# One-core graph network layer: the last edges moved into the last chunk, and a tail in five parts whose residual is doubled and summed in PSUM

## The reference

```python
msg = x[src] + edge_attr
agg = jax.ops.segment_sum(msg, dst, num_segments=N)
h = jax.nn.relu(agg @ W1 + b1) @ W2 + b2
mu = jnp.mean(h); var = jnp.mean((h - mu) ** 2)            # over everything
h = (h - mu) * jax.lax.rsqrt(var + EPS) * ln_w + ln_b
mean = jnp.mean(h, axis=0); sub = h - gn_ms * mean          # over the nodes
h = sub * jax.lax.rsqrt(jnp.mean(sub ** 2, axis=0) + EPS) * gn_w + gn_b
out = layernorm(x + (gelu(h) + x))                          # per node, over 128 features
```

## Time and profile before

| | |
|---|---|
| median of 3 runs | 765.46 us (765.35 to 767.17) |
| the profiled execution's own time | 766.76 us |
| its span in the trace | 764.9 us |
| TensorE busy | 686.3 us, 90% of the span |
| VectorE busy | 637.0 us, 83% |
| ScalarE busy | 429.0 us, 56% |
| GpSimd busy | 101.3 us, 13% |
| mean granted clock of TensorE | 0.962 of full speed |

### The profile page before, as it was taken

The page is one execution under the profiler, slowest core; times in us unless marked ns, Lnnn a source line. Parts: engine busy times, 40 slices in busy tenths (PEclk is TensorE's granted clock), DMA queues, the critical chain, the costliest instruction groups (busy, mean ns, idle before and its releaser), DMA issues.

```text
span 764.9 us, 25427 instructions
## 1 busy us (share of the span) xinstructions
PE 686.3 (90%) x9447; PEld 624.5 (82%) x9447; DVE 637.0 (83%) x1074; ACT 429.0 (56%) x968; POOL 101.3 (13%) x68
## 2 busy tenths in 40 slices
PE   1975999999999999999999999999999999989640
PEld 1964888999889998899988999889998889968530
DVE  5786989899898998989989899898998989335684
ACT  0934466655666556664566645756457564234475
POOL 2043210111101111011110112101111011000000
PEclk9986999999999999999999999999999999989975
DMA  7957465256652566525665255662556626260006
GB/s 171 298 189 247 145 196 183 97 177 214 200 185 88 181 210 205 180 89 184 206 209 187 79 190 198 209 193 75 194 193 209 202 72 199 76 168 0 0 0 167
DMA packets 88984, 123.60 MB, mean 162 GB/s; under 512 B 8572, under 2 KB 84446, under 8 KB 88763
## 3 DMA queue, kind: packets, MB, share of 16 engines
q1 hardware_dynamic: 82220, 116.30, 47.5%
q0 software_dynamic: 5744, 5.38, 2.6%
q10 hardware_dynamic: 1000, 1.65, 0.8%
HBM read 119.23 MB, written 4.03 MB: 161 GB/s over the span
## 4 chain that ended last, share of the span: by engine, by line
PE 75%; ACT 11%; DVE 6%; issue 3%; DMA 3%; DVEq 1%; ACTq 0%; SPq 0%; POOLq 0%
PE bank L800 39%; PE bank L765 17%; PE bank L713 9%; ACT counts L586 6%; PE bank L850 3%; PE bank L860 3%; PE bank L727 2%; ACT below L530 2%; DMA begins<-listed,tile_slot 2%; DMA agg<-in_dst_dram 1%; ACT pool_m L669 1%; DVE pool_m L1087 1%; DVE x_lo L1028 1%; PE bank L742 1%; PE bank L887 1%
## 5 line engine op out<-in xcount | busy, mean ns | idle before, releaser
L586 ACT CAST counts<-bank 128x490 fp32r<-128x490 f32 x600 | 320.5, 606 | 239.0 <-PE bank L765 235.9
L800 PE MATMUL bank<-counts,x_hi 128*128 128x250 f32 x1225 | 307.7, 291 | 8.7 <-ACT counts L586 8.6
L800 PE MATMUL bank<-counts,x_lo 128*128 128x250 f32 x1225 | 292.8, 279 | 0.0
L800 PEld LDWEIGHTS bank<-counts,x_hi 128*128 128x128 f32 x1225 | 230.9, 189 | 14.4 <-ACT counts L586 14.4
L1087 DVE TENSOR_TENSOR pool_m<-value_row,turned_lo 128x3328 bf16<-128x3328 bf16 (+1 forms) x125 | 229.1, 1833 | 12.0 <-PE bank L765 10.8
L800 PEld LDWEIGHTS bank<-counts,x_lo 128*128 128x128 f32 x1225 | 232.4, 190 | 0.0
L765 PE MATMUL bank<-pool_m 128*128 128x98 bf16 x3125 | 194.9, 210 | 7.8 <-DVE pool_m L1087 7.7
L765 PEld LDWEIGHTS bank<-pool_m 128*128 128x128 bf16 x3125 | 158.5, 99 | 27.2 <-issue 11.6
L1087 DVE TENSOR_TENSOR pool_m<-value_row,turned_key 128x2548 bf16<-128x2548 bf16 (+1 forms) x125 | 179.6, 1437 | 0.0
L713 PE MATMUL bank<-edges,onehot 128*32 128x128 f32 x3228 | 121.6, 285 | 5.1 <-DMA edges<-in_edge_attr_dram 3.0
L479 POOL DMA_INDIRECT near<-listed,row_slot x27 | 53.6, 1987 | 501.1 <-DVE row_slot L1049 459.5
(11 more groups left out here) (154 smaller groups left out, 442.0 us busy)
## 6 DMA issues: line engine op xcount, KB each, us to landing
edges<-in_edge_attr_dram SPq DMA_DIRECT2D x134, 768.0 KB, 6.1
out_dram<-pool_m SPq DMA_DIRECT2D x6, 512.0 KB
agg<-in_dst_dram SPq DMA_DIRECT2D x1, 768.0 KB
agg<-in_src_dram ACTq DMA_DIRECT2D x1, 768.0 KB
listed<-agg ACTq DMA_DIRECT2D x1, 768.0 KB
begins<-listed,tile_slot POOLq DMA_INDIRECT x28, 4.1
near<-listed,row_slot POOLq DMA_INDIRECT x27, 4.3
pool_m<-in_L_gnn_W_dram SPq DMA_DIRECT2D x2, 128.0 KB, 2.7
```

The source lines that it names most:

```text
L586: nc.scalar.copy(counts[:, :, at:at + NODES], cps[k % RING][:, 0:NODES * NT].rearrange("p (n q) -> p q n", q=NT)).then_inc(banks_free, 1)
L800: last = nc.tensor.matmul(sps[:, 0:CHUNK], part[:, q, :], counts[:, q, at:at + CHUNK], start=(q == 0 and part is x_hi), stop=(q == NT - 1 ...
```

## The change

- The last two groups of edges and the fast path's check are put between the 49 pairs of products of the last chunk (`finish_edges`). VectorE makes their masks before the check's counts, and adds both groups before the last chunk.
- The last part of the edge features, and the last tile of the output, are transferred in two pieces each.
- x is not loaded again. TensorE multiplies `x_hi` and `x_lo` by a diagonal matrix of twos (`double`) into a ring of seven PSUM banks, and adds the transposed gelu onto it: a matmul with `is_transpose=True` and `start=False` in place of `nc.tensor.transpose`. VectorE takes the statistics straight from PSUM (`measure`), and `finish` is gone.
- The layernorm's scales are made in five parts (blocks 0 to 2, 3 to 5, 6 to 8, 9 to 10, 11 to 12). GpSimd raises to the power -0.5, and makes the shifts; ScalarE scales blocks 0, 2, 4, 5, 6, 7, 9 and 11, VectorE blocks 1, 3, 8, 10 and the last tile, reading PSUM, and SyncE writes block by block.
- In the affine, GpSimd's power stands in place of ScalarE's square root and VectorE's reciprocal. The statistics of the first 24 chunks are joined first and the last chunk's are taken from PSUM; the chain of one-column operations is rearranged.

```diff
 BLOCK = 4
+RINGED = 7
+ACT_SCALES = {7: (0,), 8: (2,), 9: (4,), 11: (5,), 12: (6, 7, 9, 11)}
+DVE_SCALES = {6: (1,), 7: (3,)}
+DVE_LAST = (8, 10)
+BY_ACT = sum(ACT_SCALES.values(), ())
+BY_DVE = sum(DVE_SCALES.values(), ()) + DVE_LAST
+PARTS = ((0, 3), (3, 6), (6, 9), (9, 11), (11, 13))
+EVEN_LAST = 96
...
-        ops = [banks[4], sps, banks[0], banks[1]]
+        ys = [banks[i] for i in (4, 5, 7, 0, 1, 2, 3)]
+        twice = counts[:, 0, 0:P]
...
-                sp.dma_start(edges[0:REST_P, 2 + k, 0:HP], edge_rest[:, k * HP:(k + 1) * HP]).then_inc(tail_loaded, 16)
+                for a, b in ((0, REST_EVEN), (REST_EVEN, REST_P)):
+                    sp.dma_start(edges[a:b, 2 + k, 0:HP], edge_rest[a:b, k * HP:(k + 1) * HP]).then_inc(tail_loaded, 16)
...
-            sp.dma_start(xs[:, 0:NT - 1, :], x[0:(NT - 1) * P, :].rearrange("(t p) d -> p t d", p=P)
-                         ).then_inc(xs_loaded, 16)
-            sp.dma_start(xs[0:LAST, NT - 1, :], x[(NT - 1) * P:N, :]).then_inc(xs_loaded, 16)
...
+            def wait_scaled(k):
+                if k in BY_ACT:
+                    sp.wait_ge(act_out_ready, BLOCK * (BY_ACT.index(k) + 1))
+                else:
+                    sp.wait_ge(out_ready, BLOCK * (BY_DVE.index(k) + 1))
...
+            for k in range(BLOCKS):
+                wait_scaled(k)
+                sp.dma_start(out[k * BLOCK * P:(k + 1) * BLOCK * P, :].rearrange("(t p) d -> p t d", p=P),
+                             xs[:, k * BLOCK:(k + 1) * BLOCK, :]).then_inc(out_stored, 16)
+            sp.wait_ge(out_ready, BLOCK * len(BY_DVE) + 1)
+            for a, b in ((0, EVEN_LAST), (EVEN_LAST, LAST)):
+                sp.dma_start(out[(NT - 1) * P + a:(NT - 1) * P + b, :], xs[a:b, NT - 1, :]).then_inc(out_stored, 16)
...
+            pool.wait_ge(power_ready, 1)
+            for n, (base, to) in enumerate(((st[:, 3:4], st[:, 4:5]), (st[:, 9:10], st[:, 9:10]))):
+                pool.wait_ge(roots_in, n + 1)
+                pool.tensor_tensor(to, base, half_power[:, 0:1], ALU.pow).then_inc(roots_out, 1)
+            for n, (a, b) in enumerate((a * BLOCK, min(b * BLOCK, NT)) for a, b in PARTS):
+                total, scale, half = lnsum[:, a:b], rstd[:, a:b], half_power[:, 0:b - a]
+                pool.wait_ge(ln_stats, b)
+                pool.tensor_tensor(total, lnstats[:, a:b, 1], lnstats[:, a:b, 4], ALU.add).then_inc(sums_made, 1)
+                pool.wait_ge(sums_made, 2 * n + 1)
+                pool.tensor_tensor(total, total, half, ALU.mult).then_inc(sums_made, 1)
+                pool.wait_ge(sums_made, 2 * n + 2)
+                pool.wait_ge(roots_in, n + 3)
+                pool.tensor_tensor(scale, scale, half, ALU.pow).then_inc(roots_out, 1)
+                pool.wait_ge(roots_out, n + 3)
+                pool.tensor_tensor(lnshift[:, a:b], total, scale, ALU.mult).then_inc(scales_ready, 1)
...
-            for k, (a, b) in enumerate(((st[:, 4:5], turn_ps[:, 1:2]), (st[:, 9:10], st[:, 9:10]))):
-                act.wait_ge(root_in, k + 1)
-                nc.scalar.activation(a, b, ACT.Sqrt, bias=st[:, 21:22]).then_inc(root_out, 1)
...
+            def scale_block(k):
+                act.wait_ge(scales_ready, 1 + max(i for i, (a, b) in enumerate(PARTS) if a <= k))
+                for t in range(BLOCK):
+                    at = k * BLOCK + t
+                    nc.scalar.activation(xs[:, at, :], ys[k % RINGED][:, t * P:(t + 1) * P], ACT.Identity,
+                                         scale=rstd[:, at:at + 1], bias=lnshift[:, at:at + 1]).then_inc(act_out_ready, 1)
...
+            for k in range(BLOCKS + 1):
+                width = BLOCK * P if k < BLOCKS else LAST
+                if k >= 2:
+                    act.wait_ge(out_turned, k - 1)
+                nc.scalar.activation(gelu[:, k % 2, 0:width], h[:, k * BLOCK * P:k * BLOCK * P + width],
+                                     ACT.Gelu_apprx_tanh, scale=st[:, 10:11], bias=st[:, 12:13]).then_inc(act_ready, 1)
+                for done in ACT_SCALES.get(k, ()):
+                    scale_block(done)
...
+            def finish_edges(q):
+                if q in (4, 8):
+                    k = (4, 8).index(q)
+                    begin_half(FULL - 1, k, edge_loaded[k], 16 * (GPC + USES[k] * PAIRED + 2))
+                    sum_half(k, 0, k)
+                if q == 16:
+                    turn_sums(FULL - 1, 0)
+                if q in (24, 28):
+                    k = (24, 28).index(q)
+                    begin_half(FULL, k, tail_loaded, 64)
+                    sum_half(2 + k, 1, k, subs=1)
+                if q == 34:
+                    turn_sums(FULL, 1)
+                if q == 38:
+                    pe.wait_ge(ones_ready, 1)
+                    pe.wait_ge(cover_in, 1)
+                    pe.wait_ge(keys_ready, 2 * CHUNKS)
+                    nc.tensor.matmul(turn_ps[:, 0:TURNS + 2], ones, st[:, COVER:COVER + TURNS + 2], start=True, stop=True
+                                     ).then_inc(cover_summed, 1)
...
+            def double(k):
+                if k >= RINGED:
+                    done = k - RINGED
+                    if done in BY_ACT:
+                        pe.wait_ge(act_out_ready, BLOCK * (BY_ACT.index(done) + 1))
+                    else:
+                        pe.wait_ge(out_ready, BLOCK * (BY_DVE.index(done) + 1))
+                width = BLOCK if k < BLOCKS else 1
+                for part in (x_hi, x_lo):
+                    nc.tensor.matmul(ys[k % RINGED][:, 0:width * P], twice,
+                                     part[:, k * BLOCK:k * BLOCK + width, :].rearrange("p t d -> p (t d)"),
+                                     start=(part is x_hi), stop=False, skip_group_check=True)
...
+            def turn(k):
+                pe.wait_ge(act_ready, k + 1)
+                width = BLOCK * P if k < BLOCKS else LAST
+                for t in range(0, width, P):
+                    rows = min(P, width - t)
+                    last = nc.tensor.matmul(ys[k % RINGED][0:rows, t:t + P], gelu[:, k % 2, t:t + rows], ident[:, :],
+                                            start=False, stop=True, is_transpose=True, skip_group_check=True)
+                last.then_inc(out_turned, 1)
...
+            pe.wait_ge(twice_ready, 1)
+            for k in range(3):
+                double(k)
             for k in range(2):
                 pe.wait_ge(mean_in, k + 1)
                 nc.tensor.matmul(turn_ps[:, k:k + 1], ones, st[:, k:k + 1],
-                                 start=True, stop=True, skip_group_check=True).then_inc((mean_summed, root_in)[k], 1)
-            def turn(u, count, free):
-                pe.wait_ge(act_ready, count)
-                if free is not None:
-                    pe.wait_ge(y_ready, free)
-                for t in range(BLOCK):
-                    last = nc.tensor.transpose(ops[u][:, t * P:(t + 1) * P], gelu[:, u % 2, t * P:(t + 1) * P],
-                                               ident[:, :])
-                last.then_inc(out_turned, 1)
-            for u in range(OPS):
-                turn(u, u + 1, None)
-            with pe.Fori(1, BLOCKS // OPS) as it:
-                for u in range(OPS):
-                    turn(u, it * OPS + (u + 1), it * OPS + (u + 1 - OPS))
-            pe.wait_ge(act_ready, BLOCKS + 1)
-            pe.wait_ge(y_ready, BLOCKS + 1 - OPS)
-            nc.tensor.transpose(ops[0][0:LAST, 0:P], gelu[:, 0, 0:LAST], ident[:, :]).then_inc(out_turned, 1)
+                                 start=True, stop=True, skip_group_check=True).then_inc(mean_summed, 1)
+            pe.wait_ge(hidden_ready, CHUNKS * HC)
+            pe.wait_ge(h_ready, CHUNKS)
+            for k in range(3, RINGED):
+                double(k)
+            for k in range(BLOCKS + 1):
+                if k >= RINGED:
+                    double(k)
+                turn(k)
...
-            dve.memset(st[:, 21:22], EPS)
+            for k in range(2):
+                mark_lead(FULL - 1, k)
+            add(FULL - GPC, FULL % GPC, base_of(FULL - GPC), CHUNKS)
+            put(FULL - 1)
+            for k in range(2):
+                mark_lead(FULL, k)
...
+            for g in range(FULL - 1, GROUPS):
+                add(g, g % GPC, base_of(g))
...
             flag = dve.value_load(flag_i[0:1, 0:1], min_val=0, max_val=1)
-            add_chunk(CHUNKS - 1, FULL - 1, 0)
+            add_chunk(CHUNKS - 1, GROUPS, 0)
             dve.wait_ge(chunk_added, CHUNKS + 1)
-            for g in range(FULL - 1, GROUPS):
-                add(g, g % GPC, base_of(g))
-            dve.wait_ge(edges_added, GROUPS + 2)
...
+            dve.tensor_scalar(twice, ident[:, :], 2.0, None, ALU.mult).then_inc(twice_ready, 1)
+            step(dve.memset(joined[:, 0:1], float((CHUNKS - 1) * CHUNK)))
+            dve.memset(half_power, -0.5).then_inc(power_ready, 1)
...
-            keep(CHUNKS - 1, 0, CHUNKS)
-            dve.wait_ge(h_stats, CHUNKS)
...
```

(65 more changed lines are left out.)

146 lines of the change are left out of this document (18 added, 128 removed).

## The result

The changed kernel takes **753.93 us** (4 runs, 753.40 to 756.05) against 765.41: a ratio of 0.985, with a 95% interval of 0.9826 to 0.9873. That is 11.5 us gained where 16.3 were forecast. The profiled execution took 756.05 us, with a span of 754.2. That is 10.7 less than the 764.9 of the kernel before.

| stretch | before | after | forecast for after |
|---|---|---|---|
| start to the last chunk's first product | 654.63 | 658.52 | 654.63 |
| from there to the layers' first product | 19.12 | 17.04 | 16.22 |
| the layers | 45.8 | 43.15 | 42.9 |
| the layers' end to the first gelu | 7.34 | 7.66 | 7.0 |
| first gelu to the span's end | 38.0 | 27.83 | 27.8 |

The account below looks back on a forecast made before the run. After 654 us it saw TensorE bounding last chunk and layers, a VectorE chain before gelu, and VectorE the tail. Gains of 2.9 + 2.9 + 0.3 + 10.2 = 16.3 us off 765.46 gave 749.2 us, range 744.5 to 753.5.

Parts of the forecast that it names:

- Step 1: Last chunk: with the last edges inside it, the layers start at 670.85 instead of 673.75, -2.9 us.
- Step 2: Layers: TensorE, idle for only 0.8 us before them, runs at 2.4 GHz from their start, -2.9 us.
- Step 3: Affine, layers' end to first gelu: table load moved ahead, powers of 0.4 us on GpSimd, 7.0 us against 7.3, -0.3 us.
- Step 4: Tail, first gelu to the span's end: ScalarE bounds it, 27.8 us against 38.0, -10.2 us.
- If GpSimd's rows pass 1 us: Sign that the forecast is wrong: a GpSimd operation longer than 1 us in the trace.
- the other two: Signs of being wrong: TensorE waits inside the last chunk, or VectorE scales last by over 1 us.
- The clock at the layers' start: Rival: TensorE's clock falls there all the same, +2.9 us, 752.1 us; chance 0.12.
- at 0.27: Rival, tail: ScalarE's scales from PSUM cost 0.27 us each, 3.8 us less, 745.4 us; chance 0.12.
- GpSimd the bound: Rival: the power is so slow that GpSimd bounds the kernel; 768 us at 5 us a power; chance 0.04.
- Power costs 1.5 us: Rival: GpSimd's power takes 1.5 us, +2.2 us before gelu, parts still hidden, 751.4 us; chance 0.13.
- The rival on the transposes' clock: Rival: the tail stays at 1.2 GHz, so its transposes run slower, +1.3 us, 750.5 us; chance 0.08.

Follow-up runs that it names:

- `tail_only`: The changed kernel with the last edge groups put back behind the last chunk, as before: 756.97 us, ratio 0.9882.
- the second profile: The profile of the changed kernel run once more, unaltered: 753.32 us, ratio 0.9847, with a tail of 26.92 us.

## Why the prediction was right or wrong

**Where the work begins: the step that failed.** "Up to 654 us nothing is changed, and no term below comes from there." Nothing of the code is changed there, but the two first transfers are issued within a hundredth of a microsecond of each other, and the changed build turns their order round. That costs 1.5 to 2.4 us by the medians and 2.3 by the mean of the profiles. It is the largest term of the 4.8 us missing, and no row that I read bore on it: I had looked at nothing ahead of 654 us.

**Step 1, -2.9: measured -2.1.** The mechanism holds: one add between chunk and layers, TensorE idle for 0.78 us. Two terms were mis-sized. The edge products were put at 2.08 and, "by the same rate", 0.23 for the last 6; they take 0.79 twice and 0.77 twice, 3.12 in all. The trace of before had the answer in its list in order of time, where the last short half is a row of its own, which the chain of waits that I used doesn't have:

```profile
668.82 0.84 PE L713 MATMUL bank<-edges,onehot 128*32 128x128 f32 x6
```

And the changes of kind, for which I allowed 0.5, cost 0.95, nearly my worst case: the 98 products take 12.59 in their eight pieces, where they took 11.64 in a row. Most of that lies behind edge products, as the pieces of 8 show. The two turns were cheaper, 0.22 each and not 0.43: 15.42 + 0.81 + 0.45 - 0.42 = 16.26, as measured.

**Step 2, -2.9: measured -2.65.** The clock stayed at 1.00, and the layers took 43.15 to 43.17 us, in every kernel with the edges inside the chunk. The missing 0.25 is in the start: the second `down` begins 3.98 us after the first `up` (679.54 against 675.56), where I had 3.7 by "three times 0.84 less the overlap". And the 45.8 us from which I subtracted was at the high end: the four profiles of kernels before have 45.80, 45.83, 45.20 and 44.50, and `tail_only`, with its edges behind the chunk too, has 44.50. On the mean of the four (45.3) the step is worth 2.2.

**Step 3, -0.3: measured +0.3.** The table load lies behind the last relu, as forecast. The join of 24 chunks was seen to be on the path. The powers were mis-sized: 0.59 and 0.56 us, with 0.78 and 0.67 of waiting, against 0.4 with semaphores, and the mean input came 0.1 later than forecast. Taking the value near the one-column iota was right in kind and 0.3 too low for each, waits included.

**Step 4, -10.2: measured -10.2, partly by luck.** ScalarE bounds the tail, its last scale ends 24.04 us after the first gelu (forecast 23.4), and 3.8 follow (forecast 4.4). But the condition that I named, ScalarE without gaps from the eighth gelu on, isn't met: "GpSimd's four operations for a part (some 1 us)" take 3.2 to 3.4 us for 12 columns, because I had priced the power over a part like a one-column one. That put 2.0 us of waits into ScalarE's queue. Against it, the eighth gelu ended 7.1 us after the first, and not 7.5, and the scales cost 0.37 and not 0.39. "If GpSimd's rows pass 1 us" was one of my signs of being wrong, and it came true (2.28); the other two didn't: TensorE has no wait inside the last chunk, and VectorE ends its scales 1.1 us before ScalarE.

**The rivals.** The clock at the layers' start didn't fall. ScalarE reads PSUM at 0.37, not at 0.27. The power didn't make GpSimd the bound. "Power costs 1.5 us" was wrong for one column (0.59) and near for eight (1.64). The rival on the transposes' clock came half true: in the profile the first eight turns ran partly at a mean of 0.57 of full speed, and the tail is 0.9 us longer than in the second profile, where they ran at 1.00. The clock came back while TensorE did only transposes (one run of them from 728.80 to 732.50), as windows of the changed kernel show:

```profile
731.00:732.00 1.00, 1.00 (x6) 0.86 (x7) 0.93 (x7) 0.65 (x2) 0.64 (x3) 0.50 0.00 0
732.00:733.00 1.00, 0.66 (x5) 0.42 (x4) 1.00 (x7) 1.00 (x2) 1.00 (x1) 0.96 0.00 0
```

The rule of the Trainium skill, "TensorE: Matmul & The Clock Gate", section on PE-mode transpose, that transposes don't count as busy for the clock, isn't borne out by these fp32 transposes; the page's own figures there are for bf16.

**The sum.** Of the 4.8 us, about 2.3 are the start, 0.8 step 1, 0.6 step 3, and 0.3 step 2 with another 0.5 for its reference; the last 0.3 are within what four runs tell. The range of 744.5 to 753.5 held all that I had bounded and ended 0.4 us short, for a term that wasn't in it.

## What to carry to other kernels

A change far from the start can still move it: compare the first transfers, their order and the first waits of both traces before any other stretch, and where two queues start within some hundredths of a microsecond, order them with a wait. Price GpSimd's power by its columns, and not its operations by their count, and work out when each consumer's first element is ready. Edge products that fill one group of 32 columns cost as much as those that fill four (0.77 us against 0.79).

## What the hardware did that I hadn't expected

- Two loads of 768 KB, issued by two engines within 0.01 us of each other (0.17 where a wait orders them), go one behind the other: in the first 4 us one queue moved 32 to 48 packets and the other none, in all profiles but one (there 4). In the kernel before, all 64 packets of the first load are moved by 5 us, and none of the other.
- GpSimd's power takes about 0.4 us and 0.16 for each column (0.56 to 0.59, 1.17, 1.64, 2.28 and 2.91 us for 1, 5, 8, 12 and 16 columns of 128 rows), where GpSimd's other operations on the same tiles take 0.20 to 0.26, and a product in the power's place 0.19 to 0.21 for 1 to 12.
- Six edge products take 0.77 us where 24 take 0.79. By the code, a full half puts six on each of four groups of 32 columns, and a short one all six on one group. From the two times it follows that the four groups ran side by side, or nearly so.
- TensorE's clock fell at different points of the same work: in the changed kernel 2 us after the first gelu in one execution and 4 us before it in another.
